# Output attention as eight more units of the head pipeline, with the result stored batch by batch

## The reference, cut to what matters

```python
def gat_layer(x, graph, W, b):
    h = x @ W
    s = jnp.einsum('bnd,bmd->bnm', h, h) * graph
    s = jnp.where(s == 0.0, NEG_INF, s)
    a = jax.nn.softmax(s, axis=2)
    return jnp.einsum('bnm,bmd->bnd', a, h) + b
heads = jax.vmap(lambda W, b: gat_layer(flow_x, graph, W, b))(Wh, bh)
cat = jnp.moveaxis(heads, 0, 2).reshape(B, N, H * D)
x = jax.nn.leaky_relu(cat, negative_slope=0.01)
out = gat_layer(x, graph, W_out, b_out)
return jax.nn.leaky_relu(out, negative_slope=0.01)
```

## Time and profile before

| What | Value |
|---|---|
| median of 3 runs | 2573.38 us |
| the profiled execution: its time / its span | 2569.81 us / 2568.1 us |
| head stage, first to last masked tile (L559) | 938.9 to 2246.3 us |
| output stage, first to last masked tile (L220) | 2291.5 to 2542.6 us |
| busy in the span: TensorE, VectorE, ScalarE, GpSimd | 85%, 83%, 57%, 24% |

### The profile page before, as it was taken

One profiled execution on the slowest core, in us unless ns is written; L12 is line 12 of the kernel. 1 busy time (PEld: TensorE's weight loads), 2 busy tenths in 40 slices (PEclk: granted clock), 3 DMA queues, 4 the chain that ended last, 5 costly groups with the idle time before them and its releaser, 6 DMA issues. The chain is left out here.

```text
span 2568.1 us, 57991 instructions
## 1 busy us (share of the span) xinstructions
PE 2194.8 (85%) x24542; PEld 1479.4 (58%) x24542; DVE 2119.2 (83%) x2873; ACT 1470.0 (57%) x2342; POOL 611.1 (24%) x362
## 2 busy tenths in 40 slices
PE   3868778367758579999999999999999999969887
PEld 2644446345537456666666666666666666646665
DVE  7558854788864549999999999999999999947775
ACT  2522222298952136666666666666666666647664
POOL 0049960000000012332333333233332332210000
PEclk8969999679979769999999999999999999989998
DMA  3000000000000031111010010100101000010000
GB/s 113 1 1 0 0 0 1 1 1 1 1 2 1 0 70 43 34 33 38 27 43 27 27 43 32 46 27 27 43 27 43 27 32 30 27 42 1 1 1 33
DMA packets 61879, 60.79 MB, mean 24 GB/s; under 512 B 50368, under 2 KB 51520, under 8 KB 60992
## 3 DMA queue, kind: packets, MB, share of 16 engines
q1 hardware_dynamic: 61632, 57.21, 7.4%
HBM read 44.34 MB, written 4.46 MB: 19 GB/s over the span
## 5 line engine op out<-in xcount | busy, mean ns | idle before, releaser
L627 ACT ACTIVATE x_sb<-x_sb,hid_neg_max 128x1024 f32<-128x1024 f32 x512 | 587.0, 1151 | 236.9 <-DVE hid_neg_max L559 236.9
L559 DVE CUSTOM_DVE_ANT_0 x_sb<-ps_score,adj_mask,row_scale 128x1024 f32<-128x1024 f32 x512 | 639.5, 1249 | 14.4 <-PE ps_score L466 13.8
L569 DVE STREAM_TRANSPOSE hid_weights_t<-x_sb 128x1024 f32<-128x1024 f32 x512 | 634.7, 1240 | 12.8 <-ACT x_sb L627 11.6
L484 PE MATMUL ps_low<-hid_weights_t,hid_x_rep 32*64 32x256 f32 x16384 | 506.7, 380 | 1.3 <-ACT hid_hidden L642 1.3
L466 PE MATMUL ps_score<-hid_y_hi,hid_xs 128*128 128x512 f32 x1024 | 463.8, 453 | 8.3 <-DVE hid_neg_max L559 6.5
L484 PEld LDWEIGHTS ps_low<-hid_weights_t,hid_x_rep 32*64 32x64 f32 x16384 | 345.9, 131 | 139.5 <-issue 88.2
L466 PE MATMUL ps_score<-hid_y_lo,hid_xs 128*128 128x512 f32 x1024 | 403.4, 394 | 0.0
L694 POOL TENSOR_TENSOR hid_z<-hid_z,hid_inv_cols 128x1024 f32<-128x1024 f32 x64 | 195.7, 3058 | 717.6 <-ACT hid_z L635 717.6
L466 PEld LDWEIGHTS ps_score<-hid_y_hi,hid_xs 128*128 128x128 f32 x1024 | 192.6, 188 | 204.1 <-issue 151.6
L466 PEld LDWEIGHTS ps_score<-hid_y_lo,hid_xs 128*128 128x128 f32 x1024 | 193.7, 189 | 42.2 <-issue 14.8
L687 POOL TENSOR_TENSOR hid_y_lo<-hid_y_wide,hid_y_hi 128x1024 fp32r<-128x1024 f32 x64 | 153.4, 2398 | 237.0 <-ACT hid_y_wide L622 237.0
(11 more groups left out here) (322 smaller groups left out, 3638.0 us busy)
## 6 DMA issues: line engine op xcount, KB each, us to landing
hid_inv_cols<-hid_inv_rows SPq DMA_DIRECT2D x64, 512.0 KB, 3.7
hid_x_rep<-h_sb SPq DMA_DIRECT2D x128, 64.0 KB, 2.6
adj_rows<-in_adj SPq DMA_DIRECT2D x8, 512.0 KB, 7.1
x_sb<-in_x SPq DMA_DIRECT2D x2, 1024.0 KB, 6.3
x_saved<-x_sb SPq DMA_DIRECT2D x1, 2048.0 KB, 8.6
x_sb<-x_saved SPq DMA_DIRECT2D x1, 2048.0 KB, 7.8
out_x<-x_sb SPq DMA_DIRECT2D x1, 2048.0 KB, 6.3
hid_inv_rows<-hid_row_inv SPq DMA_DIRECT2D x64, 4.0 KB, 1.4
```

The source lines that it names most:

```text
L484: ins = pe.matmul(m.ps_low[c * F:(c + 1) * F, a, 0:NT * Q], x_rep[a * Q:(a + 1) * Q, g // HEADS % 2, b, :], weights_t[a * Q:(a + 1) * Q, g ...
L559: dve.tensor_tensor_reduce(ring[:, i % RING, :], m.ps_score[:, i % 2, :], m.mask[:, t, :], m.row_scale[:, t, g // HEADS:g // HEADS + 1], HUGE,
L569: dve.transpose(weights_t[:, g % 2, :, t, :], ring[:, i % RING, :].rearrange("p (b j) -> p b j", j=Q)).then_inc(tile_turned, 1)
L627: act.activation(ring[:, i % RING, :], ring[:, i % RING, :], ACT.Exp, scale=-1.0, bias=neg_max[:, g % 2, t:t + 1], accum_out=row_sum[:, g ...
```

## The change

`out_attention` and `store` are removed. `hidden_attention` becomes `last_attention` with 72 units: units 64 to 71 are the output attention of batches 0 to 7. The core of the diff:

```diff
+    HEAD_UNITS = B * HEADS
+    UNITS = HEAD_UNITS + B
...
+        def turn_back(p):
+            if p % HEADS == 2 and HEADS < p < HEAD_UNITS + HEADS:
+                return p // HEADS - 1
+            return None
...
+            def store_flags(b):
+                sp.wait_ge(flags_ready, 2 * b + 2)
+                sp.dma_start(col_rows[b].rearrange("(t p) -> p t", p=P), col_flag[:, b, :],
+                             allow_slow_non_contiguous=True).then_inc(col_stored, 16)
+
+            def spread_flags(b):
+                sp.wait_ge(col_stored, 16 * (b + 1))
+                if b >= 2:
+                    sp.wait_ge(mask_built, (b - 1) * NT)
+                sp.dma_start(col_mask[:, b % 2, :],
+                             col_rows[b].rearrange("(a n) -> a n", a=1).to_broadcast([P, N]))\
+                    .then_inc(col_spread, 16)
+
+            def load_x(b):
+                if b >= 2:
+                    sp.wait_ge(stored, 16 * (b - 1))
+                else:
+                    sp.wait_ge(hidden_ready, HEAD_UNITS)
+                sp.dma_start(x_in[:, b % 2, :, :],
+                             x_saved.rearrange("p (t b f) -> p t b f", b=B, f=F)[:, :, b, :])\
+                    .then_inc(x_in_loaded, 16)
+
+            def store(b):
+                sp.wait_ge(final_ready, b + 1)
+                sp.dma_start(d["out"][:, :, b, :], x_in[:, b % 2, :, :]).then_inc(stored, 16)
...
-            for g in range(UNITS):
+            for g in range(UNITS + 2):
+                if g < UNITS:
...
+                if g == HEAD_UNITS - 4:
+                    sp.wait_ge(rows_back, 1)
+                    sp.wait_ge(values_ready, HEAD_UNITS - HEADS)
+                    load_rows(0, out_rows_loaded)
+                if HEAD_UNITS <= g < UNITS - 1:
+                    b = g - HEAD_UNITS + 1
+                    sp.wait_ge(rows_back, b + 1)
+                    sp.wait_ge(values_ready, g)
+                    load_rows(b, out_rows_loaded)
+                if g and turn_back(g - 1) is not None:
+                    store_flags(turn_back(g - 1))
+                if HEAD_UNITS - 2 <= g < UNITS - 2:
+                    spread_flags(g - HEAD_UNITS + 2)
+                if g >= HEAD_UNITS + 2:
+                    store(g - HEAD_UNITS - 2)
+                if HEAD_UNITS <= g < UNITS:
+                    load_x(g - HEAD_UNITS)
```

```diff
+            def rows_of_out(b):                      # TensorE, t == 6 of unit turn_back: 8 matmuls
+                pe.wait_ge(out_added, (HEADS - 1) * (b + 1))
...
             def project(g):                          # TensorE, t == 7
+                if g >= HEAD_UNITS:
+                    pe.wait_ge(rows_back, g - HEAD_UNITS + 1)
+                    for part in range(2):
+                        ins = turn_rows(g - HEAD_UNITS, part, 2 + part)
+                    ins.then_inc(y_ready, 1)
+                    return
...
+            def final_rows(g):
+                pe.wait_ge(bias_ready, 2)
+                pe.wait_ge(z_normed, g + 1)
+                pe.wait_ge(out_taken, HEAD_UNITS)
+                pe.matmul(m.ps_low[:, 0, :], ones[:],
+                          out_bias[:].unsqueeze(1).to_broadcast([P, NT, F]), start=True, stop=False)
+                for t in range(NT):
+                    ins = pe.matmul(m.ps_low[:, 0, t * F:(t + 1) * F], z[:, t * P:(t + 1) * P], fold[:],
+                                    start=False, stop=(t == NT - 1))
...
+            def find_largest(b):
+                dve.wait_ge(rows_back, b + 1)
+                dve.tensor_reduce(largest[:, b, :], m.h[:, :, b, :], AX, ALU.max, apply_absolute_value=True)\
+                   .then_inc(flag_step, 1)
+
+            def build_mask(i):
+                b, t = i // NT - HEAD_UNITS, i % NT
+                if t == 0:
+                    dve.wait_ge(col_spread, 16 * (b + 1))
+                if i >= HEAD_UNITS * NT + 2:
+                    dve.wait_ge(masked_ready, i - 1)
+                dve.tensor_tensor(masks[:, t % 2, :], m.mask[:, t, :], col_mask[:, b % 2, :], ALU.min)\
+                   .then_inc(mask_built, 1)
...
                         turn_tile(i - 1)
                     if i + 2 < TILES:
                         mask_tile(i + 2)
+                    if HEAD_UNITS * NT <= i + 3 < TILES:
+                        build_mask(i + 3)
...
+                    if t == 3 and HEAD_UNITS <= g + 1 < UNITS:
+                        copy_lo(g + 1)
...
+                act.activation(hidden[:, 0:HALF], m.ps_low[:, 0, :], ACT.Relu, scale=0.99)
+                act.activation(share[:], m.ps_low[:, 0, :], ACT.Identity, scale=0.01).then_inc(hidden_read, 1)
...
+            def add_x(g):
...
+                link(pool.tensor_tensor(x, x, share[:], ALU.add))
+                pool.tensor_tensor(x, x, hidden[:, 0:HALF], ALU.add).then_inc(final_ready, 1)
```

More of the change, by code:

```diff
@@ L365, in hidden_attention @@
         inv_rows = nc.dram_tensor("hid_inv_rows", (2, P, NT), F32).ap()
+        masks = sb("masks", [P, 2, N], BF16)
+        x_in = wz[:].rearrange("p h d -> p (h d)").rearrange("p (k t f) -> p k t f", k=2, f=F)
+        col_mask = sb("col_mask", [P, 2, N], BF16)
+        col_flag = sb("col_flag", [P, B, NT], BF16)
+        row_flag = sb("row_flag", [P, B, NT])
+        largest = sb("largest", [P, B, NT])
+        fold = sb("fold", [P, F])
+        ones = sb("ones", [P, P], F32R)
+        out_bias = sb("out_bias", [P, F], F32R)
+        col_rows = nc.dram_tensor("hid_col_rows", (B, N), BF16).ap()
         gram_ready = sem("gram_ready")
@@ L395, in hidden_attention @@
         out_added = sem("out_added")
+        rows_turned = sem("rows_turned")
+        rows_back = sem("rows_back")
+        flag_step = sem("flag_step")
+        flags_ready = sem("flags_ready")
+        col_stored = sem("col_stored")
+        col_spread = sem("col_spread")
+        mask_built = sem("mask_built")
+        bias_cleared = sem("bias_cleared")
+        bias_loaded = sem("bias_loaded")
+        bias_ready = sem("bias_ready")
+        x_in_loaded = sem("x_in_loaded")
+        final_step = sem("final_step")
+        final_ready = sem("final_ready")
+        stored = sem("stored")
         def wide(lo):
@@ L509, in _ @@
             for part in range(2):
-                turn_rows(0, part)
+                turn_rows(0, part, prep_bank(0, part)).then_inc(x_turned, 1)
             pe.wait_ge(weights_loaded, 16 * len(w.loads))
@@ L527, in _ @@
                         score(g * NT + t + 2)
-                    if t == 0 and g >= 2:
-                        if n < B and u in (2, 3):
-                            pe.wait_ge(x_split, 2 * n + u - 1)
-                        head_out(g - 2)
+                    if t == 0:
+                        if n < B and u in (4, 5):
+                            pe.wait_ge(x_split, 2 * n + u - 3)
+                        if g and turn_back(g - 1) is not None:
+                            pe.wait_ge(rows_back, turn_back(g - 1) + 1)
+                        if 2 <= g < HEAD_UNITS + 2:
+                            head_out(g - 2)
+                        if g >= HEAD_UNITS + 2:
+                            final_rows(g - 2)
                     if 2 <= t < 6 and 1 <= g <= UNITS:
                         values(g - 1, t - 2)
-                    if t == 6 and n < B and u in (1, 2):
+                    if t == 6 and n < B and u in (3, 4):
                         pe.wait_ge(z_ready, g)
-                        turn_rows(n, u - 1)
-                    if t == 6 and g >= 2:
+                        turn_rows(n, u - 3, prep_bank(n, u - 3)).then_inc(x_turned, 1)
+                    if t == 6 and turn_back(g) is not None:
+                        pe.wait_ge(z_ready, g)
+                        rows_of_out(turn_back(g))
+                    if t == 6 and 2 <= g < HEAD_UNITS + 2:
                         project_out(g - 2)
@@ L558, in mask_tile @@
                     dve.wait_ge(tile_turned, i - RING + 1)
[L559 to L560 removed]
+                if g < HEAD_UNITS:
+                    mask, scale = m.mask[:, t, :], m.row_scale[:, t, g // HEADS:g // HEADS + 1]
+                else:
+                    b = g - HEAD_UNITS
+                    dve.wait_ge(mask_built, b * NT + t + 1)
+                    mask, scale = masks[:, t % 2, :], row_flag[:, b, t:t + 1]
+                dve.tensor_tensor_reduce(ring[:, i % RING, :], m.ps_score[:, i % 2, :], mask, scale, HUGE,
                                          ALU.add, ALU.min,
@@ L598, in _ @@
                         mask_tile(i + 2)
+                    if HEAD_UNITS * NT <= i + 3 < TILES:
+                        build_mask(i + 3)
                     if t == 1 and 1 <= g <= UNITS:
                         invert(g - 1)
-                    if t == 2 and g >= 2:
+                    if t == 2 and 2 <= g < HEAD_UNITS + 2:
                         leaky(g - 2)
-                    if n < B and t == 7 and u in (1, 2):
-                        split_rows(n, u - 1)
```

(17 more changed lines are left out.)

378 lines of the change are left out of this document (93 added, 285 removed).

## The result

The changed kernel takes 2611.6 us, the median of 4 runs (2604.01 to 2615.81), against 2572.15 for the kernel before beside it (4 runs, 2570.41 to 2574.27): a ratio of 1.0149 (95% interval 1.0127 to 1.017). It is slower by 39 us, and 88 us above the forecast. The profiled execution took 2604.01 us, with a span of 2602.2.

What follows compares the result with a forecast made beforehand. TensorE and VectorE share the head unit's bound; SP's loads set six output periods of 30.3 us. With head-stage extras, 4 us for flags and the tail, the span is 2518.6 us, 49.5 less; off the median, 2523.9 (range 2480 to 2552).

Steps and rivals of the forecast that it cites:

- rival (a): Output units: flags land before VectorE asks, so no stall; units of 24.0 us, not 30.3, total 2482 us; chance 12%.
- six waits behind the loads: Iterations 64 to 69: VectorE waits 6.3 us for the flags, six times, because SP issues 16 loads first.
- the flag stores: Two-byte stores of the column flags: hidden in the head stage, +4 us once in iteration 67 (1 to 12).
- The flags: Step pricing each store's 1,024 two-byte runs: 3.2 us, hidden in the head stage, +4 us once in iteration 67.
- Rival (c): Two-byte stores hold SP's queue and make the kernel slower; below 25 us each costs only iteration 67's place; chance 4%.
- The unit without a wait: New output unit on VectorE: 18.64 + 0.12 + eight mask builds at 0.65 us = 24.0 us.
- Loads before spread: SP's order in the output stage: 12.0 us of loads delay the spread, giving six periods of 30.3 us.
- `rows_of_out` with `find_largest`: Extra work in the head stage: 1.3 us for each of seven batches, 9 us (5 to 12).
- From the last inversion but one to the last masked tile: Near the kernel's end: 9.9 us without `leaky` and with three builds, 9.14 before; reaches 2490.3 us.
- The end from there: Tail from the last masked tile to the span's end: 28.3 us, with `final_rows` at 1.5; reaches 2518.6 us.
- Rival (b): Mask builds on VectorE start 1.16 us apart, not 0.65: 23.5 us more, 2547 us; chance 17%.
- rival (d): Output units: waits leave TensorE idle and lower its clock; put at nothing, at most 6 us; no chance of its own.

Runs made afterwards that it cites:

- kernel 3: The change with flags stored as 128 runs of 16 bytes and spread ahead of the loads: 2506.43 us, ratio 0.9732 to the kernel before.
- kernels 1: The change with flags stored as 128 runs of 16 bytes, not 1,024 of two bytes: 2543.79 us, ratio 0.9884 to the kernel before.
- kernels 2: The change with the flags spread ahead of the 16 loads, two-byte stores kept: 2571.92 us, ratio 1.0002 to the kernel before.
- experiment 4: The change with SyncE waiting for the landing right behind each two-byte flag store: 2628.5 us in a single run.
- experiment 6: Kernel 2 with the two-byte flag store issued on ScalarE's queue: 2577.89 us, ratio 1.0018 to the kernel before.
- experiment 8: Kernel 2 without most value matmuls of the unit behind each store (112 of 128 left out): 2507.13 us, ratio 0.9746 to the kernel before.
- experiment 11: Kernel 3 with GpSimd's work behind the heads cut to eight columns or less, builds kept: 2475.51 us, ratio 0.9628 to the kernel before.

## Why the prediction was wrong

The forecast of 2523.9 us was a sum of three terms, and each has been measured by itself:

| Term | Forecast | Measured | By |
|---|---|---|---|
| all but the two below, rival (a)'s time | 2482.1 | 2506.4 | kernel 3 |
| six waits behind the loads | 37.8 | 37.4 to 39.7 | kernels 1 and 3, change and 2 |
| the flag stores | 4 | 65.5 to 67.8 | kernels 2 and 3, change and 1 |
| sum | 2523.9 | 2611.6 | the change |

**The step that failed is "The flags".** It has two statements, and both fell. "64 for each of 16 engines make 3.2 us" used the queue's mean packet of 928 bytes (57.21 MB / 61,632), which holds no write of two bytes. It is 14.3 us at the one place where the landing was read (experiment 4). "In the head stage this hides behind the 18 us in which SP issues nothing" named the wrong cover. SyncE issues nothing there, but TensorE fetches instructions all the time, 256 in a block, and in the value phase it uses up 64 value matmuls and as many weight loads in 3.03 us (2228.96 to 2231.99 in the trace after). This is the larger error: had 14 us been put in with the same cover, the sum would have risen by 10 us for iteration 67, and not by 64.

**Rival (c) had the sign and the culprit, not the mechanism.** It let the stores hold SyncE's queue, from 25 us on, and concluded "below 25 us it costs nothing". At 14 us they cost 68: 56 behind the seven stores of the head stage, and 11.5 in iteration 67 (44.4 against 32.9 for its neighbours). The 56 have nothing to do with SyncE's order: no inverse stands behind a store there, and in experiment 6 TensorE pauses as before with the store on another queue. In experiment 8 TensorE needs few instructions, and the loss is gone. Only in iteration 67 does the queue count, since the spread stands behind the store. Its 4% was computed from a threshold that belonged to another resource.

**The unit without a wait** was put at 24.0 us and came to some 27.4 in kernel 3 (23.6 to 24.7 with GpSimd light). The build's own duration was right (0.68 us). What I left out is that the builds wait for GpSimd: 25 us in the eight units of kernel 3 (experiment 11). By its profile the first term of the table is 31 us too low (24 in the medians): 20 in the last six units, 6 in iterations 62 and 63 (26.0 and 28.7 us, not 23.2 and 25.2), 7 in the end, and 2 less in the head stage. In the change itself five of the six units behind loads are 30.9 to 33.4 us long (30.3 forecast), and the one with the store 44.4. The Trainium skill, "GPSIMD Engine Reference" (Specifications), lists GpSimd's way to SBUF as shared with VectorE when a VectorE instruction has two inputs in SBUF; kernel 3's rows and experiment 11 agree, and I hadn't weighed it.

**The right steps.** Loads before spread, on a queue that waits for its own issues: 12.1 us of issue, six waits, 37.4 to 39.7 us by experiments 1 to 3. In front of the first builds stand waits of 5.62, 6.88, 6.44, 7.05 and 6.44 us, and one of 17.99 in iteration 67 (forecast 6.3, and about 10 once). `rows_of_out` with `find_largest` cost 0.8 us a batch (21.15 against 20.36) and not 1.3. From the last inversion but one to the last masked tile it was 9.8 us (9.9 forecast). The end from there took 34.2 us and not 28.3: the last `final_rows` took 3.0 us in place of 1.5, and the last `normalise` ended 3.7 us later than my rows gave. Rival (b), the build at 1.16 us, is out by its median of 0.68; rival (d), the clock, looked in the wrong place: it falls furthest in the pauses behind the stores (0.54, 0.63), and what that costs by itself no run separates.

What stays open: why a small write to DRAM is so slow, how its price falls with size, and why it varies from 5.5 to 15 us a store. The records show the packets over within 3 us, and no event for what follows but the late blocks.

## What to carry to other kernels

Price a transfer by its smallest run and by where it ends, not by the queue's mean packet, and keep runs of a few bytes out of DRAM: reorder on an engine that has room, or store in the order in which the partition holds the data. When a transfer is called hidden, list everyone who uses the DMA engines at that time; a TensorE stream of small matmuls is one of them, though no instruction of the program shows it. And read the durations of one operation one by one before its mean is used as a price: an engine that waits for another in the middle of an instruction looks busy.

## What the runs showed of the hardware

- 1,024 two-byte runs to DRAM take 14.3 us to land; 1,024 more of them to SBUF cost nothing measurable. Behind such a store a 4 KB transfer of another queue needs 12.16 us in place of 1.4, and TensorE's next block of 256 instructions is late (12.0 to 24.2 us behind the store, against 6.6 to 16.9), so that it runs out of instructions.
- A 16-bit `tensor_tensor` of 128x1024 in SBUF takes 0.68 us, and up to 3.4 us beside a GpSimd instruction; the long ones end some 0.55 us behind it.
- A matmul over one row (1x512) between score matmuls adds 0.53 us to the stream, where those over 128 rows start 0.23 us apart.
- A ScalarE copy of 128x1024 16-bit values that writes them at a stride of 128 takes 4.82 us; an exponential over 128x1024 float32 values takes 1.15.
